# Local attention's loop with four items a turn in place of two, its stages in new slots, and waits for all three pieces of W1

## What is computed

```python
for i in range(6):
    x = attn_layer(shift_tokens(x), Wqkv[i], q_scale[i], k_scale[i], Wo[i]) + x
    x = ffn_layer(shift_tokens(x), ln_g[i], ln_b[i], W1[i], b1[i], W2[i], b2[i]) + x

def attn_layer(x, Wqkv, qs, ksc, Wo):          # 16 heads of 64
    q, k, v = split(x @ Wqkv)                  # 128 -> 3 * 1024
    q, k = l2norm(q) * qs, l2norm(k) * ksc     # then rotary tables on q and k
    sim = einsum("bhwie,bhwje->bhwij", q, look_back(k)) * 8    # windows of 32
    return softmax(masked(sim)) @ look_back(v) @ Wo

def ffn_layer(x, g, bln, W1, b1, W2, b2):      # inner 341
    a, gate = split(layernorm(x) @ W1 + b1)
    return a * gelu(gate) @ W2 + b2
```

## Time and profile before

| | |
|---|---|
| median of 3 runs | 5213.06 us (5210.61 to 5216.11) |
| the profiled execution | 5206.96 us, of which span 5205.1 us |
| PE matmul busy | 4391.0 us (84%) |
| DVE, ACT, POOL busy | 3970.9 (76%), 3747.0 (72%), 3313.1 us (64%) |
| first item's projection starts | 510 us from the span's start |
| last W2 of the transformer added | 4373 us |
| DMA | 169.24 MB, mean 33 GB/s |

### The profile page before, as it was taken

The page is one execution under the profiler, slowest core; times in us unless marked ns, Lnnn a source line. Parts: engine busy times, 40 slices in busy tenths (PEclk is TensorE's granted clock), DMA queues, the critical chain, the costliest instruction groups (busy, mean ns, idle before and its releaser), DMA issues. The chain is left out here.

```text
span 5205.1 us, 133673 instructions
## 1 busy us (share of the span) xinstructions
PE 4391.0 (84%) x45166; PEld 3298.7 (63%) x45166; DVE 3970.9 (76%) x6890; ACT 3747.0 (72%) x11543; POOL 3313.1 (64%) x2504
## 2 busy tenths in 40 slices
PE   6986888888888898888888888888898886778776
PEld 3554677667767676776777767776676774444443
DVE  4776887878777788787878878887787783777776
ACT  2554787877877778777877778787787786656663
POOL 0111877767777788777877777777787772444444
PEclk9998999999999999999999999999999997778777
DMA  1000111111111121111111111111111110000000
GB/s 25 6 5 21 40 47 35 41 41 51 40 41 35 41 55 41 35 41 45 51 35 40 39 47 46 41 40 35 45 45 41 35 41 17 2 3 2 3 3 4
DMA packets 118558, 169.24 MB, mean 33 GB/s; under 512 B 26563, under 2 KB 44422, under 8 KB 118022
## 3 DMA queue, kind: packets, MB, share of 16 engines
q1 hardware_dynamic: 109246, 160.92, 11.7%
q10 hardware_dynamic: 8776, 0.45, 0.1%
HBM read 20.79 MB, written 2.10 MB: 4 GB/s over the span
## 5 line engine op out<-in xcount | busy, mean ns | idle before, releaser
L1372 POOL TENSOR_TENSOR b_w<-b_w,b_vt 128x512 f32<-128x512 f32 x768 | 983.5, 1287 | 728.1 <-DVE b_ss L1288 374.0
L1376 POOL TENSOR_TENSOR b_rn<-b_ssm,all_neg_half 128x16 f32<-128x16 f32 x384 | 1150.3, 2996 | 32.0
L1174 ACT ACTIVATE b_Pr<-ps,b_nm 128x96 f32<-128x96 f32 x3072 | 1002.3, 352 | 0.6
L1060 PE MATMUL ps<-b_Whi,b_xlo 128*128 128x512 f32 x1152 | 603.2, 524 | 149.0 <-issue 110.4
L1174 ACT ACTIVATION_READ_ACCUMULATOR b_Pr<-ps,b_nm 128x1 f32 x3072 | 676.3, 220 | 0.0
L989 PE MATMUL ps<-all_ident,b_w 128*128 128x128 f32 x3072 | 502.4, 291 | 172.1 <-ACT b_qkT L1144 107.9
L1026 PE MATMUL ps<-all_ident,b_Pr 128*96 128x128 f32 x3072 | 491.4, 285 | 145.3 <-DVE b_Pr L1335 136.3
L1144 ACT ACTIVATE b_qkT<-ps 128x512 f32<-128x512 f32 x768 | 469.0, 611 | 175.6 <-PE ps L989 174.8
L1341 DVE TENSOR_REDUCE b_nm<-ps 128x8 f32<-128x768 f32 x384 | 367.1, 956 | 297.7 <-PE ps L1015 297.5
L1193 ACT ACTIVATE b_sq<-ps 128x512 f32<-128x512 f32 x768 | 477.1, 621 | 145.3 <-PE ps L1062 145.2
L1216 ACT ACTIVATE b_PT<-ps 96x512 f32<-96x512 f32 x768 | 459.4, 598 | 169.0 <-PE ps L1026 168.7
(11 more groups left out here) (259 smaller groups left out, 9670.6 us busy)
## 6 DMA issues: line engine op xcount, KB each, us to landing
b_V<-b_Vraw SPq DMA_DIRECT2D x384, 192.0 KB, 2.6
b_V<-b_Vraw SPq DMA_DIRECT2D x384, 128.0 KB, 2.3
b_V<-b_Vraw SPq DMA_DIRECT2D x192, 64.0 KB, 2.2
b_Wraw<-in_L_ffn_Wqkv SPq DMA_DIRECT2D x36, 256.0 KB, 3.2
b_Wo<-in_L_ffn_Wo SPq DMA_DIRECT2D x6, 512.0 KB, 3.7
a_xtok<-in_L_attn_hidden_states SPq DMA_DIRECT2D x16, 128.0 KB, 2.1
out<-c_xout SPq DMA_DIRECT2D x16, 128.0 KB, 1.8
b_W<-in_L_ffn_W SPq DMA_DIRECT2D x6, 341.0 KB, 3.3
```

The costliest lines, as they stand in the source:

```text
L1060: nc.tensor.matmul(ps[:, F_BANK[k % 2]], s.xlo[:, pf, rows], s.Whi[:, cols], start=True, stop=False)
L1174: last = nc.scalar.activation(s.Pr[:, r % 2, j, i], ps[:, S_BANK[j], i * KEYS:(i + 1) * KEYS], ACT.Exp, bias=s.nm[:, r, j, i:i + 1], accum ...
L1372: nc.gpsimd.tensor_tensor(rows, rows, s.vt[:, i % 4], ALU.add).then_inc(s.pool_add, 1)
L1376: nc.gpsimd.tensor_tensor(s.rn[:, j], s.ssm[:, j], g.neg_half[:, 0:HB], ALU.pow).then_inc(s.pool_r, 1)
```

## The change

The loop `inner` makes four steps a turn in place of two, 3 turns a layer in place of 6. The tables of slots are new. Where SP, ACT and DVE waited for the piece of W1 that was the last, they now wait for the newest use of each spare bank among all three pieces, since piece 2 isn't the last any more; DVE gets such a wait before it overwrites `lp`, the biases that ACT reads with W1.

```diff
--- before.py
+++ after.py
@@ -713,26 +713,26 @@
 SLOTS = 32
 ROUND = SLOTS // ROUNDS
 
-QK_SLOT = {0: (0, 0), 3: (0, 2), 6: (1, 0), 8: (1, 2), 15: (0, 1), 17: (0, 3), 22: (1, 1), 24: (1, 3)}
-V_SLOT = {14: (0, 4), 20: (1, 4), 29: (0, 5), 31: (1, 5)}
-ROTATE_LAG, ADD_LAG = 2, 0
+QK_SLOT = {0: (0, 0), 2: (0, 2), 6: (1, 0), 8: (1, 2), 16: (0, 1), 17: (0, 3), 22: (1, 1), 24: (1, 3)}
+V_SLOT = {15: (0, 4), 21: (1, 4), 29: (0, 5), 30: (1, 5)}
+ROTATE_LAG, ADD_LAG = 2, 2
 CHUNKS = (0, 2, 4, 1, 5, 3)
 CONVERT_SLOT = {0: (0, 1), 4: (2,), 8: (3,), 10: (4,), 12: (5,)}
 
-LATE_SLOT = {1: (0, 1), 2: (0, 3), 6: (1, 1), 9: (1, 3)}
-WO_SLOT = (11, 13)
-W1_SLOT = {5: 0, 16: 1, 19: 2}
-XT_SLOT, XN_SLOT, W2_SLOT = 22, 31, 29
-TRANSPOSE_SLOT = {22: (0, 2), 25: (1, 2), 26: (1, 0), 27: (0, 0)}
+LATE_SLOT = {0: (0, 3), 4: (0, 1), 6: (1, 3), 7: (1, 1)}
+WO_SLOT = (11, 12)
+W1_SLOT = {5: 0, 17: 2, 21: 1}
+XT_SLOT, XN_SLOT, W2_SLOT = 21, 31, 29
+TRANSPOSE_SLOT = {22: (0, 0), 26: (1, 2), 27: (1, 0), 28: (0, 2)}
 READ_LAG = 0
 
-SCORE_LAG, EXP_LAG, SCALE_LAG, TURN_LAG, VALUE_LAG, COPY_LAG = 0, (2, 5), 8, (9, 11), 15, 14
-
-RES_SLOT, STATS_SLOT, END_SLOT, SPLIT_SLOT = 11, 23, 28, 7
-DVE_NORM_SLOT = {29: 2}
+SCORE_LAG, EXP_LAG, SCALE_LAG, TURN_LAG, VALUE_LAG, COPY_LAG = 0, (4, 5), 8, (8, 11), 14, 15
+
+RES_SLOT, STATS_SLOT, END_SLOT, SPLIT_SLOT = 14, 24, 31, 8
+DVE_NORM_SLOT = {27: 2}
 DVE_LATE_NORM_SLOT = {4: 3}
-POOL_NORM_SLOT = {5: 0, 11: 1}
-GELU_SLOT, RSTD_SLOT, GATE_SLOT = 22, 21, 18
+POOL_NORM_SLOT = {7: 0, 16: 1}
+GELU_SLOT, RSTD_SLOT, GATE_SLOT = 21, 23, 19
 
 
 def piece_slots():
@@ -813,10 +813,12 @@
         body(Step(n, n % 2, items[0], items[2], items[3], items[4], convert=n == -1))
 
     def inner(l):
-        with engine.Fori(1, NB // 2 - 1) as pair:
-            n, half = NB * l + 2 * pair + 1, NB // 2 * l + pair
-            body(Step(n, 1, (l, 2 * pair + 2), (l, 2 * pair), (l, 2 * pair - 1), (l, 2 * pair - 2), half))
-            body(Step(n + 1, 0, (l, 2 * pair + 3), (l, 2 * pair + 1), (l, 2 * pair), (l, 2 * pair - 1), half + 1))
+        with engine.Fori(0, (NB // 2 - 2) // 2) as four:
+            for of_four in range(2):
+                pair = 2 * four + 1 + of_four
+                n, half = NB * l + 2 * pair + 1, NB // 2 * l + pair
+                body(Step(n, 1, (l, 2 * pair + 2), (l, 2 * pair), (l, 2 * pair - 1), (l, 2 * pair - 2), half))
+                body(Step(n + 1, 0, (l, 2 * pair + 3), (l, 2 * pair + 1), (l, 2 * pair), (l, 2 * pair - 1), half + 1))
 
     for n in range(-1, 3):
         whole(n)
@@ -935,9 +937,9 @@
                         for tt in range(TT):
                             spread_values(f, half, tt)
                     if step.edge == 2 and half == 0:
-                        b, uses = step.spare(("w1", 2))
-                        sp.wait_ge(s.spare_full[b], uses + 1)
-                        sp.sem_inc(s.spent, 1)
+                        for b, uses in step.latest([("w1", c) for c in range(3)], False):
+                            sp.wait_ge(s.spare_full[b], uses + 1)
+                            sp.sem_inc(s.spent, 1)
                         load_w1(step.front[0])
                 if step.edge == 3:
                     b, uses = step.spare(("w2", 0))
@@ -1215,8 +1217,8 @@
                             wait(act, s.pv_done, ROUNDS * item + r)
                             nc.scalar.activation(s.PT[KEY_ROWS, p % 2], ps[KEY_ROWS, T_BANK], ACT.Copy).then_inc(s.pt_ready, 1)
                     if step.ffn is not None and step.odd and slot == GELU_SLOT:
-                        b, uses = step.spare(("w1", 2))
-                        act.wait_ge(s.spare_free[b], uses + 1)
+                        for b, uses in step.latest([("w1", c) for c in range(3)], False):
+                            act.wait_ge(s.spare_free[b], uses + 1)
                         nc.scalar.activation(s.hgate[:], s.hgate[:], ACT.Gelu).then_inc(s.gelu_done, 2)
 
             phase_b_steps(act, body)
@@ -1268,6 +1270,9 @@
                         kept.then_inc(s.lp_ready, 1)
                 if step.ffn is not None:
                     lu = known(step.ffn[0])
+                    if ("w1", 0) in step.uses_before:
+                        for b, uses in step.latest([("w1", c) for c in range(3)], True):
+                            dve.wait_ge(s.spare_free[b], uses + 1)
                     nc.vector.tensor_scalar_mul(s.lp[:], g.lparam[:, bass.ds(lu, 1), 2:9].rearrange("p a k -> p (a k)"), 1.0).then_inc(s.lp_ready, 1)
 
                 def rotate(at):
```

## The result

The changed kernel takes 4978.25 us (median of 4 runs, 4976.13 to 4979.67), the kernel before 5214.59 beside it on the same chip (5210.61 to 5218.21). The ratio is 0.9548, with a 95% interval of 0.9536 to 0.9559, so 4.5% less time. The profiled execution took 4979.67 us, span 4977.9, which is 227 less than that of before (forecast: 194).

What follows compares the result with a forecast made beforehand. PE, 84% busy, was taken as the bound, with time won where it stands still in local attention. Turns 71, slots 104 and conversion steps 19 sum to 194 us, giving 5019 us; own range 4960 to 5080, 0.8 range 4930 to 5125.

Steps and rivals of the forecast that it cites:

- the scale's wait: PE's wait for the scaled exponentials of round 0, 1.26 us a step, goes as the scale now precedes the split.
- The wait at L991: PE's wait at the late transposes for the late normalisation, said to rise from 0.63 to 1.26 us a step.
- the low clock behind the Gelu: PE's clock at 0.62 of full for 4.5 us in odd steps, expected gone, 1.5 us won each.
- Turns: Inner-loop jumps fall from 30 at 4.85 us to 12 at 6.19, 71 us won.
- Rival 4: A jump's price doubles with the body to 12.4 us, so turns don't pay; 5093 us, chance 0.1.
- Slots: New slot order in 48 pairs of steps, 1.26 us from the scale plus 0.9 from odd steps, 104 us won.
- Gelu's wait: PE's 2.33 us wait behind the Gelu in odd steps keeps its length but splits into some 1.5 and 1.
- rival 2: The wait behind the Gelu goes as well, 306 us won in all; 4907 us, chance 0.15.
- Conversion steps: In five steps `values` precedes the transposes, so loads of Wqkv come 3.8 us earlier; 19 us won.
- W1 waits: Added waits of SP, ACT and DVE on W1 pieces, met long before; 0 us, 6 if uncovered.
- Rival 1: Only the turns pay; the next dependency takes back the slots' 104 us; 5123 us, chance 0.2.
- Rival 3: The late normalisation governs the step, the rotation's 1.78 us landing on PE in 96 steps; 5294 us, chance 0.05.

Runs made afterwards that it cites:

- e1_turns: The kernel before with only the new loop, four steps a turn in place of two; 5119.75 us, ratio 0.9831.
- e2_slots: The changed kernel with the two-step loop back, so new slots and W1 waits alone; 5065.45 us, ratio 0.9727 to the kernel before.
- e7: The changed kernel with the exponentials' lags back at 2 and 5 in place of 4 and 5; 5067.82 us, ratio 0.9733 to the kernel before.
- e11_waits: The kernel before with only the three added waits on W1's pieces; 5198.3 us, ratio 0.9993.
- e4_split: The kernel before with the split of the next activations at DVE slot 8 in place of 7; 5202.95 us, ratio 0.9992.
- h1_piece_early: The kernel before with a step's second piece at slot 2 in place of 3, its rotation ahead of the late normalisation; 5199.23 us, ratio 0.9993.
- e8: The changed kernel with the late normalisation ahead of the second rotation on DVE again; 5101.61 us, ratio 0.9801 to the kernel before.
- e5_inner_flat: The changed kernel with the inner loop written out, leaving four jumps between layers; 4918.94 us, ratio 0.9452 to the kernel before.
- g1_all_flat: The changed kernel with the inner loop and the loop over layers both written out, no jumps; 4904.01 us, ratio 0.9427 to the kernel before.

## Why the prediction was right, and where it was off

The direction and the likeliest case held: 4978 lies in its own range of 4960 to 5080. Of its checks, the 18 branches, DVE's gap (some 4 us announced, 2.9 to 3.4 in the changed kernel), the scale's wait and the earlier loads came as announced. Two did not. The wait at L991 is 0.4 us a step and not near 1.3, and the low clock behind the Gelu is still there in 11 of 46 odd steps. The clean pair is on the edge: steps 16 and 17, with which 72.4 was worked out, take 72.68 us on the mean over five layers, but inside the loop a clean pair takes 71.23, just below the 71.3 that was set as the bound.

- **Turns: forecast 71, measured 87 (e1_turns).** The wrong step is "steps 16 and 17 have no jump near them", used as the clean pair for both prices. They lie between layers, and an odd step inside the loop is 0.7 us shorter in the old slots. The old jump costs 5.4 (4.85 in the forecast), and 30 times the difference is the whole miss. The new one costs 6.1 in the old slots and 5.5 in the new (I took 6.19); the dearer price was the right choice. The Trainium skill says in "Runtime: NRT & Kernel Launch", "Instruction fetch mechanics", that a taken branch out of the pages that are held has to fetch its target first; the trace agrees in kind, as DVE goes on 3.1 us behind the inner branch now. Rival 4 is out.
- **Slots: forecast 104, measured about 130 in 48 pairs.** A pair with a jump is 76.54 us in e2_slots against 79.26 before (30 pairs each), so 2.7 a pair where I had 2.16. A clean even step gained 0.5 us (0.63 in the forecast), a clean odd one 2.1 (1.53). The sum was near by luck, since three of its terms were wrong. The scale's wait went as forecast.
  - The late normalisation is waited for 0.4 us (39.2 / 87) and not 1.26. In step 36 it ends at 8.1 us and not at 8.45, as it is no longer held up by POOL's add (last section), which rows 8 had in them and I took for its own duration; and PE comes at 7.9 and not at 7.19, of which 0.36 is a wait on "issue" ahead of the scores and the rest is not explained.
  - The clock, entered as 1.5 won in every odd step, was worth 0.35: ACT was busy beside it all through. And it did not go in all of them.
  - What pays for the odd steps is that ACT's copies now stand ahead of the table's reload and the exponentials, which the prediction had read as a backlog of 0.6. In the kernel before this backlog showed as 14 waits for b_PT at L1041 (15.3 us), which are gone, or lay beside slow matmuls. e7 prices that one edit at 96 us.
- **Gelu's wait: right.** 1.4 and 0.8 us on the mean with work between, where I had 1.5 and 1; rival 2 is out.
- **Conversion steps: forecast 19, measured near 12 in e2_slots** (a step 15 with the one ahead takes 83.94 us on the mean against 88.99, less the 2.7 of a normal pair, times five). The loads of Wqkv do start 4.4 us earlier into the step (12.57 against 16.94), but PE comes earlier too and still waits 3.7 at L1028: it looks like a wait for a chain that starts with the step and not with the loads alone, which no run tested.
- **W1 waits: right, nothing** (e11_waits).
- The 130 and the 12 make 142, where e2_slots measured 141.
- **Rival 1** did not happen to the whole, but it is what happens to the parts one by one (e4_split, h1_piece_early). **Rival 3** is turned round: in the new slots it is the normalisation ahead of the rotation that costs (e8).

Not tried: each table of slots by itself in the changed kernel (W1, V pieces, moments, the second normalisation), so which of them keeps POOL's gated layer from being waited for is open.

## What to carry to other kernels

In a schedule where four engines are 64 to 84% busy, an edit that removes a wait of 100 us may bring nothing by itself and 60 to 130 us once the others are made: test slots in groups, and price a single edit by taking it out of the group. Read the price of a jump, or of anything periodic, against steps of the same kind, here steps inside the loop, not those that happen to stand beside it, and over all layers, not in one. Before a low clock is entered as a loss, look at the stretch with the low clock itself: if the engine beside it is busy all through there (ACT 4.97 of 5 us in step 9 of e1_turns), the clock may be covered until that engine is relieved; if it has gaps (4.45 in step 37 of e5_inner_flat), it is not.

## What the runs showed of the hardware

**DVE and POOL hold each other up, and the order of their starts says which one pays.** DVE's normalisation has both inputs in SBUF. In e8_late_norm it starts at 1307.84, behind POOL's add of 1307.40 (row above), and here is the DVE's row:

```profile
1307.84 1.92 DVE L1300 TENSOR_TENSOR b_w<-b_w,b_rn 128x1024 f32<-128x1024 f32 x1
```

The add took its usual 1.27, to 1308.67, and the normalisation 1.92: it is 0.7 us longer, near the 0.83 for which the add was still running. In the changed kernel it starts first:

```profile
1288.41 1.22 DVE L1300 TENSOR_TENSOR b_w<-b_w,b_rn 128x1024 f32<-128x1024 f32 x1
```

Now it takes 1.22, and POOL's add of 1288.57 takes 2.18 in place of 1.27, 0.9 longer, near the 1.06 for which the normalisation was still running. POOL's next instruction starts at 1290.72, so the time is lost and not only recorded. The scale in e8_late_norm is a third case: it starts 0.71 us before POOL's add ends and takes 0.57 longer. On the mean over 700 to 4050 us, from the kernel before to the changed one, DVE's normalisation went from 1.79 us to 1.39, POOL's add from 1.28 to 1.52. The Trainium skill, "SBUF — State Buffer", section "SBUF: two separate sides", says that the two share a pair of ports as an exclusive lock, which whoever starts first holds for the whole instruction, and that a DVE instruction with two SBUF inputs takes part in it against a POOL instruction that reads SBUF. All three cases agree with it to within 0.15 us, each a little shorter than a full block would make it. A duration in a trace can thus hold another engine's work: the 1.92 of the earlier trace rows did.

**A taken branch into a long body** holds PE 3.3 to 3.9 us at most turns, for bodies of two and four steps alike (up to 4.7 in e1_turns). DVE and ACT go on 2.7 to 3.4 us behind it with the four-step body in the changed kernel and 2.5 to 3.9 in e1_turns, but 0.2 with the two-step body; on POOL it is 0.2 in both. On DVE and ACT this time is not in the branch instruction but behind it, so a list of long instructions does not show it. In straight-line code (g1_all_flat) no such gap appeared on PE, DVE or ACT.
